# A fused attention and feed-forward kernel: feature turns moved to the down steps, the down waits split by part, one norm application a step later, a longer kept ending

## The reference

```python
paths = sigmoid(x @ Wp + bp)                       # 8 heads x 5 levels
agree = pq * pk + (1 - pq) * (1 - pk)              # per level, query against key
sim = cumprod(agree, axis=-1).sum(axis=-1) / DEPTH
attn = softmax(where(mask, -inf, sim))             # causal
x = layernorm(x + (attn @ (x @ Wv)) @ Wo)
h = silu(x @ wg.T) * (x @ wu.T)                    # 768 hidden columns, integer weights / 127
x = layernorm(x + h @ wd.T)
```

## Time and profile before

| | |
|---|---|
| median of 3 runs | 944.2 us (944.07 to 945.45) |
| the profiled execution | 944.54 us |
| its span, first to last instruction | 942.8 us |
| PE busy | 846.7 us, 90% |
| DVE busy | 480.6 us, 51% |
| ACT busy | 456.3 us, 48% |
| POOL busy | 227.6 us, 24% |
| mean granted TensorE clock | 0.973 of full speed |

### The profile page before, as it was taken

One profiled execution on the slowest core, in us unless ns is written; L12 is line 12 of the kernel. 1 busy time (PEld: TensorE's weight loads), 2 busy tenths in 40 slices (PEclk: granted clock), 3 DMA queues, 4 the chain that ended last, 5 costly groups with the idle time before them and its releaser, 6 DMA issues.

```text
span 942.8 us, 15453 instructions
## 1 busy us (share of the span) xinstructions
PE 846.7 (90%) x6146; PEld 412.6 (44%) x6146; DVE 480.6 (51%) x1021; ACT 456.3 (48%) x721; POOL 227.6 (24%) x266
## 2 busy tenths in 40 slices
PE   5399998899989999799988999899998999898984
PEld 3144355443544436344454435444363444344352
DVE  2844436445465436554275354654355552754375
ACT  2255644546355454554546454555535545364431
POOL 0021231223222232131321223122421313222222
PEclk9599999999999999999999999999999999999997
DMA  6841443140421424104431314214150043200001
GB/s 214 208 105 46 90 90 113 45 88 26 112 90 46 113 45 113 67 23 112 91 112 46 71 43 112 90 46 90 49 132 23 24 113 83 75 2 22 1 1 47
DMA packets 44362, 71.09 MB, mean 75 GB/s; under 512 B 3584, under 2 KB 21248, under 8 KB 44288
## 3 DMA queue, kind: packets, MB, share of 16 engines
q1 hardware_dynamic: 44288, 70.07, 28.4%
HBM read 53.28 MB, written 16.78 MB: 74 GB/s over the span
## 4 chain that ended last, share of the span: by engine, by line
PE 73%; DVE 9%; ACT 8%; issue 3%; DMA 3%; POOL 3%; SPq 1%; POOLq 0%; ACTq 0%; DVEq 0%
PE ctx_ps L788 14%; PE misc L823 12%; PE den_ps L788 12%; PE slot L766 11%; PE misc L833 8%; PE misc L742 7%; ACT probs L451 6%; PE misc L800 6%; POOL work L404 2%; DVE work L612 2%; PE misc L751 2%; DVE x L595 2%; DVE ctx_raw L522 1%; DMA phi_dram<-phi_lo 1%; ACT work L463 1%
## 5 line engine op out<-in xcount | busy, mean ns | idle before, releaser
L451 ACT ACTIVATE probs<-slot 128x1024 f32<-128x1024 f32 (+3 forms) x384 | 290.4, 808 | 374.5 <-PE slot L766 374.2
L766 PE MATMUL slot<-query_stack,key_stack 128*128 128x512 f16 (+3 forms) x768 | 162.8, 334 | 16.6 <-DMA query_stack<-phi_dram 15.4
L788 PE MATMUL ctx_ps<-probs,vz_sb 128*32 128x512 f32 (+3 forms) x1536 | 166.0, 504 | 10.0 <-DVE ctx_raw L522 9.7
L404 POOL TENSOR_TENSOR work<-work 128x512 f16<-128x512 f32 x96 | 112.7, 1174 | 216.5 <-ACT work L469 216.5
L788 PE MATMUL den_ps<-probs,ones 128*32 128x512 f32 (+3 forms) x1536 | 163.0, 496 | 0.0
L390 POOL TENSOR_SCALAR_AFFINE_SELECT probs<-probs 128x512 f32<-128x512 f32 x128 | 81.7, 640 | 309.2 <-ACT probs L451 308.1
L612 DVE SCALAR_TENSOR_TENSOR work<-work,misc 128x512 f32<-128x512 f32 x90 | 61.8, 686 | 165.7 <-ACT work L463 165.7
L823 PE MATMUL misc<-x1T_hi,w_parts 128*128 128x512 f16 x360 | 136.7, 380 | 1.4 <-DVE x1T_lo L602 0.9
L823 PE MATMUL misc<-x1T_lo,w_parts 128*128 128x512 f16 x360 | 136.4, 379 | 0.0
L766 PEld LDWEIGHTS slot<-query_stack,key_stack 128*128 128x128 f16 x768 | 56.9, 98 | 171.2 <-issue 121.7
L833 PE MATMUL misc<-w_parts,work 128*128 128x256 bf16 x720 | 83.7, 273 | 8.3 <-POOL work L404 8.3
(11 more groups left out here) (74 smaller groups left out, 645.3 us busy)
## 6 DMA issues: line engine op xcount, KB each, us to landing
key_stack<-phi_dram SPq DMA_DIRECT2D x64, 256.0 KB, 6.0
query_stack<-phi_dram SPq DMA_DIRECT2D x64, 256.0 KB, 6.6
xT_sb<-in_xT_dram SPq DMA_DIRECT2D x8, 1024.0 KB, 5.1
x_sb<-in_x_dram SPq DMA_DIRECT2D x8, 1024.0 KB, 5.5
out_dram<-x SPq DMA_DIRECT2D x15, 512.0 KB, 2.9
phi_dram<-phi_hi SPq DMA_DIRECT2D x16, 256.0 KB, 2.1
phi_dram<-phi_lo SPq DMA_DIRECT2D x16, 256.0 KB, 2.3
work<-in_wgT_dram SPq DMA_DIRECT2D x1, 768.0 KB, 8.1
```

Source lines behind the costliest of these rows:

```text
L404: pool.tensor_tensor(hid_lo[:, n % M1, :], hid[:, n % HSLOTS, :], hid_hi[:, n % M1, :], ALU.subtract).then_inc(hid_lo_ready, 1)
L451: act.activation(probs[:, s % P_SLOTS, 2 * p:2 * p + 2, off:CH], slot[p][:, :, off:CH], ACT.Exp).then_inc(slot_drained[p], 1)
L766: mm = pe.matmul(slot[p][:, k, off:CH], key_stack[:, h, P * j:P * (j + 1)], query_stack[:, h, CH * c + off:CH * (c + 1)], start=True, stop ...
L788: mm = pe.matmul(sums[32 * k:32 * k + 32, off:CH], w, probs[:, s % P_SLOTS, k, off:CH], start=first, stop=final)
```

## The change

Four things are altered in the tables, and one wait in the code.

- `turn_f` and `phi` for the next batch leave steps 6, 8 and 9. The two chunks of group 0 go ahead of the two downs of steps 15 and 16, those of group 1 to step 23. `phi_store` of group 0 goes from step 8 to 16, that of group 1 from step 9 to 23, and `stack` of group 0 from step 16 to 18. `stack` of group 1 stays in step 0 of the next batch.
- `apply` and `store` of the second norm's chunk 1 go from step 17 to the end of step 18.
- `down` waits for its `hid_lo` parts one by one, in its first row tile, in place of for all six.
- The last batch does one gate pair fewer in steps 21 and 22 and has it in the ending. There gate pair 5 moves behind the projection, and the norm and its application of chunk 0 move from between the gate pairs to behind the last of them.

```diff
         6: turn_x1(-1, 1) + [("load_xT", 2), ("bias", 1, 1), ("squash", 1, 1)]
-            + turn_f(1, 0, 0) + turn_f(1, 1, 0) + [("features", 1, 1)],
+            + [("features", 1, 1)],
...
-        8: gate_pair(-1, 7) + halves(-1, 6) + turn_f(1, 0, 1) + [("phi_store", 1, 0)],
-        9: gate_pair(-1, 8) + halves(-1, 7) + turn_f(1, 1, 1) + [("phi_store", 1, 1)],
+        8: gate_pair(-1, 7) + halves(-1, 6),
+        9: gate_pair(-1, 8) + halves(-1, 7),
...
-        15: down(-1, 1, 0),
-        16: [("stack", 1, 0)] + down(-1, 1, 1) + norm(1, -1, 1),
-        17: gate_pair(0, 0) + [("apply", 1, -1, 1), ("store", -1, 1)],
-        18: gate_pair(0, 1) + halves(0, 0),
+        15: turn_f(1, 0, 0) + down(-1, 1, 0),
+        16: turn_f(1, 0, 1) + down(-1, 1, 1) + norm(1, -1, 1) + [("phi_store", 1, 0)],
+        17: gate_pair(0, 0),
+        18: [("stack", 1, 0)] + gate_pair(0, 1) + halves(0, 0) + [("apply", 1, -1, 1), ("store", -1, 1)],
...
-        23: halves(0, 5),
+        23: halves(0, 5) + turn_f(1, 1, 0) + turn_f(1, 1, 1) + [("phi_store", 1, 1)],
...
     LAST_BETWEEN = {
-        17: gate_pair(0, 0) + [("apply", 1, -1, 1), ("store", -1, 1)],
-        18: halves(0, 0),
+        17: gate_pair(0, 0),
+        18: halves(0, 0) + [("apply", 1, -1, 1), ("store", -1, 1)],
         19: gate_pair(0, 1),
         20: halves(0, 1),
-        21: gate_pair(0, 2),
-        22: halves(0, 2),
-        23: [],
+        21: [], 22: [], 23: [],
...
     def ending():
-        return ([("weigh", b, NS - 3)] + gate_pair(b, 3) + [("weigh", b, NS - 2), ("weigh", b, NS - 1)] + halves(b, 3)
-                + [("normalise", b, NQ - 1)] + gate_pair(b, 4) + halves(b, 4) + gate_pair(b, 5) + halves(b, 5)
-                + project(b, 1) + norm(0, b, 1) + down(b, 0, 0) + [("apply", 0, b, 1)]
-                + turn_x1(b, 1) + down(b, 0, 1)
+        return ([("weigh", b, NS - 3)] + gate_pair(b, 2) + [("weigh", b, NS - 2), ("weigh", b, NS - 1)] + halves(b, 2)
+                + [("normalise", b, NQ - 1)] + gate_pair(b, 3) + halves(b, 3) + gate_pair(b, 4) + halves(b, 4)
+                + project(b, 1) + norm(0, b, 1) + gate_pair(b, 5) + halves(b, 5) + [("apply", 0, b, 1)]
+                + down(b, 0, 0) + turn_x1(b, 1) + down(b, 0, 1)
                 + gate_pair(b, 6) + gate_pair(b, 7) + halves(b, 6) + gate_pair(b, 8) + halves(b, 7)
-                + norm(1, b, 0) + gate_pair(b, 9) + halves(b, 8) + [("apply", 1, b, 0), ("store", b, 0)]
-                + gate_pair(b, 10) + halves(b, 9) + gate_pair(b, 11) + halves(b, 10) + halves(b, 11)
+                + gate_pair(b, 9) + halves(b, 8) + gate_pair(b, 10) + halves(b, 9) + gate_pair(b, 11) + halves(b, 10)
+                + halves(b, 11) + norm(1, b, 0) + [("apply", 1, b, 0), ("store", b, 0)]
...
             def down(b, c, s, parts):
-                pe.wait_ge(hid_lo_ready, GATES * b + M1 * (c + 1))
                 k = claim("down", b, c, s)
                 for t in (2 * s, 2 * s + 1):
                     terms = [(a, e, m) for e in range(parts) for m in range(M1) for a in (hid_hi, hid_lo)]
                     for at, (a, e, m) in enumerate(terms):
+                        if t == 0 and e == 0 and a is hid_hi:
+                            pe.wait_ge(hid_lo_ready, GATES * b + M1 * c + m + 1)
```

More of the change, by code:

```diff
@@ L180, in seq_postln_kernel @@
             turn += 1
+    TURNS = {tuple(n): at for at, n in enumerate([n for what, *n in PLAN if what == "turn_f"])}
     NORM = {tuple(n): at for at, n in enumerate([n for what, *n in PLAN if what == "stats"])}
```

4 lines of the change are left out of this document (2 added, 2 removed).

## The result

The changed kernel takes **886.35 us** (median of 4 runs, 885.52 to 886.46); the kernel before, on the same chip, 944.48 (4 runs, 944.07 to 945.45). By these medians the ratio is 0.938; the recorded one is 0.936 [0.932, 0.940]. Forecast were 893.3 us, 51.1 less than before; it is some 58 less. The profiled executions have spans of 883.8 and 942.8 us, so 59.0 us are to be accounted for.

A forecast was written before the change was run, and what follows sets the result against it. PE, busy 90% of the span, was taken as the bound, so only its idle and low-clock time could go. 9.4 + 14.8 + 6.2 + 3.8 + 5.1 + 3.1 + 4.1 + 4.6 = 51.1 us less: 893.3 us, range 886 to 908.

The forecast's parts named there:

- 9.4, 14.8, 6.2 and 3.8: Middle of the run: us gained at step 6, steps 8 and 9, the downs, and step 18.
- Step 6: First feature turn gone from step 6: its wait of 2.48 us becomes 0.90 at the gate, 9.4 us gained.
- Steps 8 and 9: Turns behind gate pairs gone: all 14.8 us of waits gained, step 10 fitting narrowly; at least some 8.
- Down: Steps 15 and 0: 6.2 us of waits for hid_lo gained; added met waits free, upper bound 9 us.
- The stacks: Group 1's stacked features arrive before step 4 needs them, with 4 us of slack; nothing charged.
- Clock: Three low-clock stretches after the step 6 waits vanish, 5.1 us; none expected behind waits of 0.9 us.
- Last batch, step 18: Wait of 2.37 us falls to 1.0 and its low clock goes: 1.38 + 1.7 = 3.1 us gained.
- First batch: Steps 6 to projection: 6.4 us earlier without the turns, 2.3 us back later, so 4.1 us gained.
- Ending: After the last projection: 5.95 us gained at the last residual, 1.3 lost at a 3.9 us stall: 4.6 us.
- the waits that came back: Rival: half the recovered waits return, at the next gate, step 10 or downs; 913 us, chance 0.19.
- the stacks were in time: Rival, slower: group 1's stacks come too late for step 4; above 946 us, chance 0.02.
- the small terms: Rival: ending and first-batch terms fail together (clock low longer, application slow); 899 us, chance 0.12.

The follow-up runs named there:

- e1: Kernel before with only the feature turns, their stores and the stacked loads moved: 903.7 us, ratio 0.956.
- e2: Kernel before with only the down's wait for hid_lo split by part: 930.47 us, ratio 0.983.
- e3: Kernel before with only the second norm's application and its store moved from step 17 to the end of step 18: 933.34 us, ratio 0.986.
- e5: Changed kernel with one feature turn (group 1, chunk 1) put back from step 23 into step 9: 894.95 us, ratio 0.946.
- e9: Changed kernel with the down's waits taken back to one for all six hid_lo parts: 892.66 us, ratio 0.944.
- e10: Changed kernel with the first gate of a chunk issuing high-part products before low-part ones, waiting for each when reached: 882.74 us, ratio 0.933.
- e6: Changed kernel with the hid_lo wait ahead of all 24 second-layer matmuls of a down instead of six: 887.17 us, ratio 0.939.
- e7: Changed kernel with group 1's turns, stores and stacked load moved behind the down of step 0: 899.04 us, ratio 0.951.
- e4: Kernel before with only the new order of the ending and its kept gate pair, one wait for all parts: 942.0 us, ratio 0.994.
- e12: e10 plus, in the last batch, chunk-0 norm statistics moved to step 2 and the ending's norm put behind gate pair 5: 879.91 us, ratio 0.930.

## Why the prediction was right in direction and wrong in size

- **The step that failed** is how the prediction priced the stalls of the middle: 9.4, 14.8, 6.2 and 3.8 are sums of recorded idle. Recorded idle was taken for the whole cost. Per undisturbed batch the recorded idle that went is 2.48 - 0.84 + 2 x 1.24 + 0.69 + 0.20 + 0.64 = 5.65 us; the period fell by 6.78. Five of these stalls went altogether, the sixth only got shorter: 1.13 / 5 = 0.23 each. The experiments give the same per stall removed: 0.24 (e1: 5.48 - 4.76, three stalls removed), 0.18 (e2: 1.25 - 0.89, two), 0.25 (e3), 0.20 (e5), 0.17 (e9), and nothing in e10, where none went. 6 x 1.13 = 6.8 us. The other terms of the middle nearly cancel: 0.4 more at the gates, 0.4 more in the seventh pair of down waits, 0.2 less for the three drops of the clock (1.64 each), and 1.2 lost to a drop that was not forecast. Together that is the excess of 6.4, within rounding.
- **What is in these 0.2 us** is shown for one place: 0.07 that the last matmul's listed end lies beyond the start of a successor that doesn't wait, and 0.12 by which the first transposes behind a stall take longer (e5). For the others only the sum was measured, and that it has the same two parts there is not shown.
- Step 6: 9.4 said; (2.48 - 0.84) x 6 = 9.8, right. Steps 8 and 9: all 14.8 taken, and nothing came back at the gate of step 10, right. At the 1.43 of e5 for each, the twelve are worth 17.2, an estimate.
- Down: a gain of the recorded 6.2, met waits free (e6). Right in kind, though the bound for them counted half of the downs. But turn and parts cover the same wait in part: alone they give 5.48, 1.25 and 0.89 with the application, 7.62; together 6.78. e9 shows how little the parts still add to a middle batch.
- The stacks: no wait, right; the slack is 1.7 to 3.4 us instead of 4 (e7).
- Clock: the three drops went, and in no middle batch did one come. One that was not forecast came behind the 2.35 us wait at 753.53: from there to the gate it is 17.02 us, and 15.85 in the traces of e1 and e6 without a drop. It cost 1.2 us. Without it the median too would lie below the range by this estimate (886.35 - 1.2 = 885.2), so that it lies inside is luck.
- Last batch, step 18: 1.07 left, clock at 1.00, 1.30 + 1.64 = 2.9 us against 3.1. First batch: 5.2 to the first gate, as worked out (from the scores of step 6 to the projection 12.5 us in place of 18.3).
- Ending: -1.3 and 5.95 were forecast, -1.1 and 6.1 measured. One stall of 3.89 (3.9 said), clock 0.68 behind it. The first residual of the last chunk comes 16.16 us behind gate pair 6; forecast were 16.47 (927.2 - 910.73), against 22.42 before. The prediction puts this down to DVE's order; with the order alone it is 18.25 (e4), for then the whole down waits for the last part. The clock at 0.72 in the last down was not forecast; in e12, where it stayed at 1.00, the residual comes at 16.15, so here it cost nothing ahead of the residual. The application behind POOL's last subtraction is fast:

```profile
849.02 2.21 DVE L593 TENSOR_SCALAR x<-x,mv,rstd 128x256 f32<-128x256 f32 x4
...
872.70 1.38 DVE L593 TENSOR_SCALAR x<-x,mv,rstd 128x256 f32<-128x256 f32 x4 [1.13 <-POOL rstd L393]
```

The first runs while POOL subtracts, the second when POOL is through: 2.21 and 1.38 us, as 2.87 and 1.38 before. The Trainium skill's page "SBUF — State Buffer", section "Who interferes with whom", says that a DVE operation in a two-port mode contends with GpSimd for a pair of ports, and that `tensor_scalar` can run in such a mode. The trace agrees at both places.
- The rivals: the waits that came back are the 0.84 at the gates, which was forecast, and no other in a middle batch; the stacks were in time, and the small terms held.

## What to carry to other kernels

Where the engine that bounds the kernel runs its instructions into each other, price a stall that will go altogether by the distance of two starts against the same pair without a wait, not by the recorded idle; short stalls are underrated most (here 0.25 recorded, 0.42 real). A wait for parts of an operand cost nothing here when it was met, so let an in-order engine wait for each part when it comes to it, and issue first the products whose operands are there first. Moving a vector step out of one wait puts it into the queue ahead of another: ask which release stands behind it at the new place before counting the gain.

## What the runs showed of the hardware that was not expected

- A wait of nearly fixed length is followed by a lower clock in some executions and not in others. Of the 24 waits of 2.47 us in the traces of before, e2, e3 and e4, 10 were (3, 3, 0 and 4), costing 1.4 to 1.7 us each (from the stalled turn of step 6 to that of step 8 it was 11.9 to 12.15 us in place of 10.49). Of the 2.35 us wait in the last batch, 4 of 11 traces had it. None of the waits of 0.84 to 1.07 us was followed by one. Two short waits close together, 0.70 and 1.26 with 0.39 us of matmuls between, were followed by one in seven of the eight traces that have them, and not in e12. So totals of kernels that keep such waits differ from run to run by more than some single edits are worth, and these were told apart by the period of an undisturbed batch. The Trainium skill's page "TensorE: Matmul & The Clock Gate", section "What's actually happening", says that the default state is throttled and that activity releases it. The traces agree behind the 3.89 us in all five that have it, and behind the waits of 2.4 us in part of the cases.
- Semaphore waits that are met ahead of matmuls cost nothing measurable: 18 more in a down left its 2.71 us to the next instruction unchanged.
- The chain from the store of the features to the last stacked load varied from 14.5 to 16.2 us within one execution (e7).
